# Row maxima from strips of 32 rows, normalisations on ScalarE, and a new order of work in a decoder layer

## Time and profile before

| | us |
|---|---|
| median of 3 runs (5989.22 to 5993.96) | 5991.21 |
| the profiled execution's own time | 5965.38 |
| its span, from the first to the last instruction | 5963.5 |
| busy in the span: PE, PEld, DVE, ACT, POOL | 5036.6, 3515.4, 4912.6, 4024.9, 5176.7 |

### The profile page before, as it was taken

One profiled execution on the slowest core, in us unless ns is written; L12 is line 12 of the kernel. 1 busy time (PEld: TensorE's weight loads), 2 busy tenths in 40 slices (PEclk: granted clock), 3 DMA queues, 4 the chain that ended last, 5 costly groups with the idle time before them and its releaser, 6 DMA issues.

```text
span 5963.5 us, 117386 instructions
## 1 busy us (share of the span) xinstructions
PE 5036.6 (84%) x40772; PEld 3515.4 (59%) x40772; DVE 4912.6 (82%) x6563; ACT 4024.9 (67%) x7680; POOL 5176.7 (87%) x4040
## 2 busy tenths in 40 slices
PE   5788888888888888888888888888888888888876
PEld 3556666666565666556566666666656566566643
DVE  3788988888888888988888888888888888888862
ACT  3676776777676777777677666767667677676651
POOL 3998999899999989999899899989999899898870
PEclk8899999999999999999999999999999999999985
DMA  3221211121211221211121111221112121111100
GB/s 103 66 65 31 72 60 65 65 68 35 68 65 60 68 68 35 65 65 63 65 68 55 45 65 64 68 65 49 50 65 67 61 68 48 52 65 63 54 11 6
DMA packets 114455, 348.74 MB, mean 58 GB/s; under 512 B 12912, under 2 KB 14704, under 8 KB 113776
## 3 DMA queue, kind: packets, MB, share of 16 engines
q1 hardware_dynamic: 113904, 341.48, 17.6%
HBM read 323.60 MB, written 17.83 MB: 57 GB/s over the span
## 4 chain that ended last, share of the span: by engine, by line
PE 33%; issue 21%; DVE 19%; ACT 13%; POOL 13%; DVEq 1%; ACTq 0%; POOLq 0%; DMA 0%; SPq 0%
DVE ring L1417 8%; POOL ring L296 7%; PE ps L1073 6%; POOL ring L305 5%; ACT ps L479 5%; PE ps L906 4%; PE ps L1025 4%; PE ps L942 3%; PE ps L969 3%; PE ps L1093 2%; DVE nmax L1464 2%; ACT probs_mem L591 2%; PE ps L1102 2%; PE ps L1108 2%; PE ps L1005 2%
## 5 line engine op out<-in xcount | busy, mean ns | idle before, releaser
L296 POOL TENSOR_TENSOR ring<-du,bc 128x512 f32<-128x512 f32 x2048 | 2747.9, 1355 | 291.4 <-PE ps L1025 182.8
L1417 DVE TENSOR_TENSOR_SCAN ring<-ps,ring 128x512 f32<-128x512 f32 x2048 | 2459.4, 1211 | 455.2 <-ACT ps L479 431.8
L305 POOL TENSOR_TENSOR ring<-ring,bc 128x512 f32<-128x512 f32 x1792 | 2389.4, 1342 | 300.9 <-DVE ring L1417 287.9
L479 ACT ACTIVATE ps<-delta,a_neg 128x254 f32<-128x254 f32 x4096 | 1770.0, 468 | 525.0 <-DVE ring L1417 519.1
L1025 PE MATMUL ps<-ident,ring 128*128 128x128 f32 x8192 | 1127.5, 284 | 83.4 <-POOL ring L305 74.3
L1025 PEld LDWEIGHTS ps<-ident,ring 128*128 128x128 f32 x8192 | 972.0, 146 | 275.1 <-issue 186.4
L906 PE MATMUL ps<-band,ident_bf 32*32 32x512 bf16 (+1 forms) x8192 | 402.5, 406 | 320.8 <-DVE nmax L1464 88.5
L1464 DVE TENSOR_REDUCE nmax<-ps 128x8 f32<-128x1536 f32 (+1 forms) x256 | 516.9, 2019 | 168.0 <-PE ps L942 166.2
L591 ACT ACTIVATE probs_mem<-ps 128x768 f32<-128x768 f32 (+1 forms) x512 | 445.4, 909 | 212.6 <-PE ps L969 208.4
L1073 PE MATMUL ps<-xt_a,w_in 128*128 128x256 f32 x2048 | 483.7, 390 | 55.9 <-ACT gate_t L550 50.0
L1093 PE MATMUL ps<-w_in,xt_a 128*128 128x256 f32 x2048 | 502.7, 401 | 15.5 <-DVE hc L1557 8.1
(11 more groups left out here) (129 smaller groups left out, 6575.2 us busy)
## 6 DMA issues: line engine op xcount, KB each, us to landing
w_in<-in_w_in SPq DMA_DIRECT2D x256, 512.0 KB, 3.7
bc<-bc_rows SPq DMA_DIRECT2D x256, 512.0 KB, 4.3
x_new<-in_x SPq DMA_DIRECT2D x32, 512.0 KB, 6.9
x_res<-in_x SPq DMA_DIRECT2D x32, 512.0 KB, 6.1
enc<-in_ctx SPq DMA_DIRECT2D x64, 256.0 KB, 4.4
out<-x_att SPq DMA_DIRECT2D x32, 512.0 KB, 2.9
w_outp<-in_w_outp SPq DMA_DIRECT2D x1, 2048.0 KB, 8.1
bc_rows<-bc_sb SPq DMA_DIRECT2D x32, 32.0 KB, 1.5
```

Of the source, the lines that this page charges most:

```text
L296: nc.gpsimd.tensor_tensor(ring[:, s % RING, :].rearrange("p (n t) -> p n t", n=2), du[:, q % 2, (ic % 2) * NT:(ic % 2 + 1) * NT].rearrange ...
L305: nc.gpsimd.tensor_tensor(ring[:, s % RING, :], ring[:, s % RING, :], bc[:, s % RS, 2:4, :].rearrange("p a t -> p (a t)"), ALU.mult).then_ ...
L479: nc.scalar.activation(ps[:, s % DAR, (n % 2) * NT:(n % 2 + 1) * NT].rearrange("p (b t) -> p b t", b=GB)[:, :, 1:T], delta[:, ic, :].rearr ...
L1417: nc.vector.tensor_tensor_scan(ring[:, s % RING, :], ps[:, s % DAR, :], ring[:, s % RING, :], 0.0, ALU.mult, ALU.add).then_inc(h_done, 1)
```

## The change

Maxima. `near(n)` takes the place of `masked()` in the first pass. The queries of a block are taken in four strips of 32; a strip a sees the 160 keys from `n * 128 + 32 * a - 64` on (`NEAR` = 160), and each strip is written to the same 160 columns of its own 32 partitions. So one mask fits all strips, and four bf16 matmuls of 32 rows x 128 columns write it (`ident4` is four 32x32 identities side by side, 2 heads x 160 columns); in the first and last block eight small ones of 32x32 cover the keys outside. The scores are 32 fp32 matmuls of 32x32 tiles in place of 8 of 32x128, and the maximum reads 4 x 2 x 160 elements in all blocks.

```diff
+            def near(n):
+                for hp in range(4):
+                    r = 32 * hp
+                    nc.tensor.matmul(ps[:, PS_ATT + hp, 0:NJ * NEAR].rearrange("p (j w) -> p j w", j=NJ),
+                                     ident4[r:r + 32, :], band[r:r + 32, 0:1, 0:NEAR].to_broadcast([32, NJ, NEAR]),
+                                     start=True, stop=False, skip_group_check=True)
+                for a, lo, hi in {0: ((0, 0, 64), (1, 0, 32)), NBLK - 1: ((2, P, NEAR), (3, P - 32, NEAR))}.get(n, ()):
+                    for hp in range(4):
+                        r = 32 * hp
+                        nc.tensor.matmul(ps[32 * a:32 * a + 32, PS_ATT + hp, 0:NJ * NEAR].rearrange("p (j w) -> p j w", j=NJ)[:, :, lo:hi],
+                                         ident_bf[r:r + 32, r:r + 32], band[r:r + 32, 3:4, 0:hi - lo].to_broadcast([32, NJ, hi - lo]),
+                                         start=False, stop=False, skip_group_check=True)
...
-                    masked()
+                    near(n)
                     for j in range(NJ):
-                        for hp in range(4):
-                            r = 32 * hp
-                            last = nc.tensor.matmul(
-                                ps[:, PS_ATT + hp, j * WIN + lo:j * WIN + hi],
-                                qk[r:r + 32, j, n * P:(n + 1) * P], qk[r:r + 32, 2 + j, at:at + hi - lo],
-                                start=False, stop=True, skip_group_check=True)
+                        for a in range(4):
+                            k0 = n * P + 32 * a - 64
+                            lo, hi = max(0, -k0), min(NEAR, H - k0)
+                            for hp in range(4):
+                                r = 32 * hp
+                                last = nc.tensor.matmul(
+                                    ps[32 * a:32 * a + 32, PS_ATT + hp, j * NEAR + lo:j * NEAR + hi],
+                                    qk[r:r + 32, j, n * P + 32 * a:n * P + 32 * a + 32], qk[r:r + 32, 2 + j, k0 + lo:k0 + hi],
+                                    start=False, stop=True, skip_group_check=True)
...
-                        ps[:, PS_ATT:PS_ATT + 4, :].rearrange("p a (j w) -> p a j w", j=NJ)[:, :, :, lo:hi],
+                        ps[:, PS_ATT:PS_ATT + 4, 0:NJ * NEAR].rearrange("p a (j w) -> p a j w", j=NJ),
```

```diff
-                        wide = a == 0 and hp == 0
-                        rows, cols = (slice(0, P), slice(0, P)) if wide else (slice(32 * a, 32 * a + 32), slice(r, r + 32))
-                        nc.tensor.matmul(ps[rows, PS_ATT + hp, :].rearrange("p (j w) -> p j w", j=2),
-                                         ident_bf[r:r + 32, cols], band[r:r + 32, a:a + 1, :].to_broadcast([32, 2, WIN]),
-                                         start=(a == 0 or hp > 0), stop=False, skip_group_check=True)
+                        nc.tensor.matmul(ps[32 * a:32 * a + 32, PS_ATT + hp, :].rearrange("p (j w) -> p j w", j=2),
+                                         ident_bf[r:r + 32, r:r + 32], band[r:r + 32, a:a + 1, :].to_broadcast([32, 2, WIN]),
+                                         start=True, stop=False, skip_group_check=True)
...
+                    pe.sem_inc(st_open, 1)
                     blks = [2 * (n % 2), 2 * (n % 2) + 1]
                     masked()
```

```diff
+            def shift(use, g, b):
+
                 dve.wait_ge(ln_rstd[use], g * GB + b + 1)
-                nc.vector.tensor_scalar(dst, src[:, b, :], ln_mv[use][:, b, 0:1], ln_rs[use][:, b:b + 1],
-                                        ALU.subtract, ALU.mult).then_inc(done, 1)
+                nc.vector.tensor_scalar(ln_nm[use][:, b:b + 1], ln_mv[use][:, b, 0:1], ln_rs[use][:, b:b + 1], -1.0,
+                                        ALU.mult, ALU.mult).then_inc(ln_shift[use], 1)
...
+            def normalise(use, g, b, dst, src, done):
+                act.wait_ge(ln_shift[use], g * GB + b + 1)
+                nc.scalar.activation(dst, src[:, b, :], ACT.Identity, scale=ln_rs[use][:, b:b + 1],
+                                     bias=ln_nm[use][:, b:b + 1]).then_inc(done, 1)
```

More of the change, by code:

```diff
@@ L363, in iteration @@
-                    times_b(g, 23)
                     times_c(g, 18)
                     times_c(g, 19)
+                    times_c(g, 20)
+                    times_b(g, 22)
+                    times_b(g, 23)
+                    times_c(g, 21)
                     times_b(g, 24)
-                    times_c(g, 20)
-                    times_c(g, 21)
+                    times_c(g, 22)
                     times_b(g, 25)
+                if p1:
+                    rstd("t", g - 1, 1)
+                if cur:
@@ L1597, in iteration @@
                     scan(g, 6)
+                if nxt:
+                    shift("a", g + 1, 1)
+                if cur:
+                    scan(g, 7)
+                if p2:
+                    router(g - 2, 0)
+                if cur:
+                    scan(g, 8)
+                if p2:
+                    router(g - 2, 1)
+                if cur:
+                    times_c(g, 7)
+                    scan(g, 9)
                 if p1:
@@ L1617, in iteration @@
                 if cur:
-                    soft_step(2, g, 2)
                     scan(g, 10)
+                if p1:
+                    mixer_add(g - 1, 1)
+                if cur:
+                    scan(g, 11)
+                    soft_step(1, g, 2)
+                if p1:
+                    shift("t", g - 1, 0)
+                if cur:
+                    scan(g, 12)
+                if p1:
+                    mixer_stats(g - 1, 1)
+                if cur:
+                    scan(g, 13)
                 if p2:
@@ L1622, in iteration @@
                 if cur:
-                    scan(g, 11)
-                    y_step(g, 0)
-                    scan(g, 12)
+                    scan(g, 14)
+                if nxt:
+                    conv(j, 0)
+                if cur:
+                    scan(g, 15)
+                if nxt:
+                    conv(j, 1)
+                if cur:
+                    scan(g, 16)
+                    scan(g, 17)
                 if p2:
@@ L1628, in iteration @@
                 if cur:
-                    scan(g, 13)
+                    times_c(g, 15)
                 if p1:
@@ L1637, in iteration @@
                 if cur:
-                    times_c(g, 15)
-                    scan(g, 16)
+                    scan(g, 19)
+                    y_step(g, 1)
+                    scan(g, 20)
                 if p1:
@@ L1674, in iteration @@
                 if cur:
-                    scan(g, 29)
+                    soft_step(3, g, 2)
+                    times_c(g, 23)
+                    scan(g, 24)
                 if nxt:
@@ L1678, in iteration @@
                 if cur:
+                    scan(g, 25)
+                    y_step(g, 2)
+                    scan(g, 26)
+                    scan(g, 27)
+                    scan(g, 28)
                     soft_step(4, g, 2)
+                if p1:
+                    shift("t", g - 1, 1)
+                if cur:
+                    scan(g, 29)
                     scan(g, 30)
-                    soft_step(2, g, 3)
+                    scan(g, 31)
+                    times_c(g, 31)
+                    scan(g, 32)
+                if nxt:
+                    conv(j, 4)
                 if p1:
@@ L1684, in iteration @@
                 if cur:
-                    scan(g, 31)
-                    times_c(g, 31)
-                    scan(g, 32)
-                if p1:
-                    attention_x(g - 1, 1)
-                if cur:
                     scan(g, 33)
+                if nxt:
+                    conv(j, 5)
                 if p1:
@@ L1714, in iteration @@
                 if cur:
-                    scan(g, 40)
-                    times_c(g, 39)
+                    scan(g, 39)
                 if p1:
@@ L1719, in iteration @@
                 if cur:
+                    soft_step(3, g, 3)
+                    times_c(g, 39)
+                    scan(g, 40)
                     scan(g, 41)
-                    scan(g, 42)
                 if p1:
@@ L1744, in iteration @@
                 if cur:
-                    scan(g, 49)
-                    y_step(g, 5)
+                    scan(g, 47)
+                    soft_step(4, g, 3)
+                    times_c(g, 47)
                 if nxt:
```

642 lines of the change are left out of this document (302 added, 340 removed).

## The result

The changed kernel takes 5707.79 us (median of 4 runs, 5698.46 to 5715.58) against 5990.22 beside it (4 runs): ratio 0.9529, 95% interval 0.9511 to 0.9548, so 282 us faster. Its profiled execution took 5703.3 us with a span of 5701.5, 262 less than the one before.

A forecast was written before the change was run, and what follows sets the result against it. It saw no always-busy engine but a chain of waits over all four; -34 - 41 + 18 - 13 - 75 - 49 = -194 us gave 5771 profiled, 5797 us with 25.8 added for the median; 8-in-10 range 5690 to 6010.

The forecast's parts named there:

- Everything tightens: Rival: DVE and PE get lighter, so POOL may reach 94% of a 168.6 us period; 5709 us, chance 0.12.
- The prices from the chain: Each engine's or line's chain time over its busy time, taken as the share of a saved microsecond that counts.
- New order: Moved softplus, `y_sum`, projections and `gate_in` on the engines' lists: taken as 0 us, both signs open.
- Maxima: Row maxima on DVE, all 256 reading 1280 elements in 1499 ns: 133 us saved, times 0.25, -34 us.
- Normalisations: Moved from DVE to ACT: DVE -178 us, priced -41; ACT +134 us at 0.70 us each, hand-over covered by order.
- Table loads: ACT changes its table 13 times an iteration instead of 14: 32 fewer loads of 1.283 us, -41 us of ACT.
- POOL: Paired powers save 44 us and fewer product meetings with DVE 43: POOL -87 us, times 0.15, -13 us.
- Scores: First-pass score groups on PE fall from 1.71 to 1.24 us: 118 us saved, times 0.64, -75 us.
- The strips run in turn: Rival: the four 32-row score strips don't overlap in fp32, so a group takes 2.67 us; 6029 us, chance 0.11.
- Issue is the limit: Rival: issuing 64 score loads and passes sets PE's time, a group taking 3.3 us; 6132 us, chance 0.04.
- Second-pass masks: PE's wide mask matmul goes, one halt of 0.31 us less in 256 groups: 79 us, times 0.62, -49 us.
- POOL holds: Rival: POOL stays at 90.6% of the period, which becomes 175 us; 5898 us, chance 0.22.

The follow-up runs named there:

- e1: The kernel before, in its old order, with the new scores, maxima over 160 keys and sixteen equal second-pass masks: -168 us.
- e7: The kernel before with the powers on POOL left out (137 us of them), the normalisation waiting for variance plus epsilon: 51 us slower.
- e2: e1 with the normalisations moved too, `shift` on DVE and the multiply on ACT, places chosen by the author: lost all that e1 had gained.
- e3: The changed kernel with its edits taken back, keeping only the new order and the softplus with `lnv`: 58 us slower than the kernel before.
- e4: The new order with new scores, maxima and masks, but normalisations on DVE and single powers: 289 us faster than e3, -62 against e1.
- e8: The changed kernel with four more of the 64 products with C an iteration on DVE instead of POOL: 10 us slower, within the intervals.
- e10: The changed kernel with a shorter softplus, max(z, 0) + ln(1 + exp(-|z|)), leaving out the rounding correction's two DVE steps and one ACT operation: gains nothing.

## Why the prediction was right, and where it was not

It said faster, 5797 us with a range of 5690 to 6010, and faster it is. The time lies in the range and outside the forecast's own 5725 to 5870; the rival *Everything tightens*, at 5709, describes it. Against its own profiled execution it forecast -194 us; -262 was measured. The other 21 us of the 89 are the 25.8 that it added for the median: the profiled execution after lies only 4.5 below its median. That the sum came so near is partly luck. By the runs in the new order it missed 58 us of loss by the order, 131 us of gain by the scores (158 against 289) and 15 by the normalisations with the pairs (36 against 51): the first error hides part of the others.

- *What bounds it.* The shares and waits were read rightly. The prices from the chain (0.15 for POOL to 0.65 for PE) held in the old order for the scores: -158 forecast, -168 in e1. They didn't for the powers (e7), nor for ACT's work (e2: +168). A share of the chain says where the time of one execution ran; in these runs it was no measure of what an edit there returns.
- **New order, "I take 0 for the new order, with both signs open".** This step failed, in its use more than in its number. The order is worth +58 or -62 us by what else is changed, and it raises the worth of the scores from 168 to 289. The sum treated all terms as independent of it, and it took PE's clock as given: the new place of the first row's groups, behind 3.3 us without work, has them at the lower level (0.54 in e3, where it was 1.00).
- *Maxima.* 1483 ns against 1499. Right.
- *Normalisations.* ACT 799 to 815 ns against 700, in all 154.6 us against 134; `shift` 38 us against 30. Inside the bounds. The cover that the prediction named held for "a" (3.8 us of ACT's idle time), less for "e" (30.0), and not for "t": the 74.3 us at `xb` are the new long wait at ACT's normalisation that it gave as a sign of being wrong. In the new order they don't reach far: the scans wait 237.8 us for decays, not above 432. In e2, at my place for them, the waits are 311 and 627.1 us, and there the gain was gone.
- *Table loads.* 418 after against 446 (the prediction's 443 leaves three single ones out): 28 fewer, not 32.
- *POOL.* The pairs are mis-sized: a call for two rows takes 1134 or 1052 ns and not one row's 770 or 596, so 17.5 us went instead of 44. Products above 1.6 us fell from 602 to 544, and the time above 1.27 us a product from 304 to 264 us, 40 against 43 assumed. Together some 57 us against 87; the page's busy time, where overlapping ends count once, fell by 66.
- *Scores.* The group has one halt less and the strips overlap, as forecast; it takes 1.41 us, not 1.24, as 64 passes need 1.17 us and not 0.98. The size was off too: the 1.71 us are two groups at the upper clock, and over all 256 the mean fell from 1.92 to 1.59, 83 us and not 118 (109 in e1, where the first row keeps its place). Within the new order, from e3 to e4, it fell from 2.16 to 1.54, 158 us: the edit is worth more there in part because the old groups would have run at the lower clock. *The strips run in turn* (2.67 us) and *Issue is the limit* (3.3 us) are out. The Trainium skill's rule in "TensorE: Matmul & The Clock Gate", "Wait — 56ns, not 53.3ns?", of some 25 ns from start to start, would make 1.6 us of the 64 passes; the trace's 1.17 us are 18 ns each and disagree.
- *Second-pass masks.* The group falls from 1.795 to 1.491 us in the mean, 0.30 against 0.31. Undone in the new order it is worth 104 us, long products included, against 49: the price, more than the size, was low. For `st_open` nothing shows.
- *POOL holds.* Refuted: its share of the period rose from 90.6% to 95%.

What stays open is why DVE's product is let in or not when it starts at the same point of POOL's, why e7 is slower, and how much of the order's worth is the clock. That POOL sets the end in the changed kernel is what its chain says (53%), and yet e8 and e10, with 128 fewer and with quicker products, were no faster. So I read it as a ring in which POOL, DVE, ACT and PE hand on, and in which each place has its own bound; no run shows that as a whole.

## What to carry to other kernels

Read an edit's worth at its own place in the period, as time between two fixed instructions, and run order and edits crosswise: here one order is worth +58 or -62 us by what it carries. Price a hand-over by what is queued behind the waiting instruction on its in-order engine; a wait of 1.9 us ahead of a block of table loads took a scan's wait from 0.9 us to 4.7. When work moves, look at the granted clock of the matmuls behind its new place. Where an edit takes the load off two engines and gains nothing, look for the group whose mean has risen.

## What the runs showed of the hardware

- A VectorE product of 128x512 floats from SBUF, started in one of GpSimd's, ends either 1.17 us later, with GpSimd's next stretched to 1.71, or only when GpSimd stops: 6.05 us behind five products in a row. Both forms come at the same point of GpSimd's product (0.63 to 0.66 us in: 4 of 32 long in the changed kernel, 32 of 32 in e10). The Trainium skill ("SBUF — State Buffer", "SBUF: two separate sides") has the port pair of the two as a lock that the first to start holds for its whole instruction. The trace agrees that one stands still, and adds that the loser can stay so over four further instructions.
- GpSimd's power takes 596 to 776 ns in the mean for 128x1 (538 at least) and 1052 to 1134 for 128x2 (687 at least).
- With 3.29 us without matmuls ahead of them, the score groups of e3 ran at a granted clock of 0.54; with 1.05 us ahead of them, those of the kernel before at 1.00. The same group took 3.20 us and 1.83.
- ScalarE's Identity over 512 columns in SBUF with two per-partition operands takes 0.80 to 0.82 us, where Exp or Ln with none takes 0.63.
